# A four-layer graph network in fp32: two row broadcasts moved from TensorE to transfers, the second layer's slope and mask moved from GpSimd to VectorE

## What is computed

```python
def L0(h, adj, W, a):                      # first layer
    Wh = h @ W.T
    s1, s2 = Wh @ a[0, :128], Wh @ a[0, 128:]
    e = leaky_relu(s1[:, :, None] + s2[:, None, :], 0.2)      # a row of s2 for all nodes
    att = softmax(where(adj == 0, -inf, e))
    return att @ Wh

def L1(x, adj, W, a_1, a_2, a_12, W_1, W_2):                  # second layer
    h = x @ W
    logits = (h @ a_1).T + h @ a_2 + (h @ a_12) @ h.T
    e = leaky_relu(logits, 0.2)
    e = where(adj > 0, e, -9e15)
    return elu(x @ W_1 + (softmax(e) @ x) @ W_2)

def L2(x, adj, ...):                       # third layer: attention with 4 heads of 32
    scores = q @ k.T * scale;  attn = softmax(where(adj | eye, scores, min))
    return relu((attn @ v) @ Wo + bo)

x = layernorm(x + L0(x)); x = layernorm(x + L1(x))
x = layernorm(x + L2(x)); x = layernorm(x + L3(x))            # L3: gated relation layer
```

## Time and profile before

| | |
|---|---|
| time, median of 3 runs | 496.18 us (496.12 to 496.77) |
| the profiled execution | 496.9 us, of it the span 495.0 us |
| PE busy | 468.4 us, 95% of the span, 3872 matmuls |
| DVE busy | 410.8 us, 83% |
| ACT busy | 428.0 us, 86% |
| POOL busy | 370.6 us, 75% |
| DMA | 26.9 MB, the 16 engines 18% busy |
| granted TensorE clock | 0.988 of full speed on average |

### The profile page before, as it was taken

How to read it: one execution, slowest core, us unless ns; L and a number is a source line. 1 busy time by engine, 2 the same in 40 slices (tenths; PEclk the granted TensorE clock), 3 DMA queues, 4 the chain that set the end, 5 groups by cost and what they waited for, 6 DMA issues and landing times. The chain is left out here.

```text
span 495.0 us, 13988 instructions
## 1 busy us (share of the span) xinstructions
PE 468.4 (95%) x3872; PEld 402.3 (81%) x3872; DVE 410.8 (83%) x1605; ACT 428.0 (86%) x1261; POOL 370.6 (75%) x736
## 2 busy tenths in 40 slices
PE   6968999999999999999999999999999999999793
PEld 5756778988888888988888888888888888877572
DVE  5657898998888998898888988898898989876653
ACT  3558999999999999999999999999999999988750
POOL 1365576788888888888888888888888888986523
PEclk9989999999999999999999999999999999999997
DMA  7211111122112221222112221221123100000011
GB/s 219 74 44 44 44 54 52 40 63 66 40 48 66 66 66 54 54 66 63 36 56 66 65 60 51 66 65 43 45 66 87 34 23 13 23 24 23 22 45 44
DMA packets 40222, 26.93 MB, mean 54 GB/s; under 512 B 2641, under 2 KB 39889, under 8 KB 40146
## 3 DMA queue, kind: packets, MB, share of 16 engines
q1 hardware_dynamic: 40146, 26.03, 18.4%
HBM read 17.63 MB, written 8.39 MB: 53 GB/s over the span
## 5 line engine op out<-in xcount | busy, mean ns | idle before, releaser
L1211 POOL TENSOR_SCALAR x<-y,minus_mean,rstd 128x128 f32<-128x128 f32 x244 | 144.8, 601 | 6.8 <-issue 5.1
L788 ACT ACTIVATE p<-p,nmax 128x256 f32<-128x256 f32 x256 | 128.5, 530 | 0.4 <-DVE nmax L981 0.4
L981 DVE CUSTOM_DVE_ANT_0 p<-ps,neg 128x256 f32<-128x256 f32 x256 | 90.7, 420 | 2.3 <-PE ps L564 2.3
L1193 POOL TENSOR_TENSOR rstd<-ve,minus_half 128x2 f32<-128x2 f32 x128 | 91.1, 712 | 0.0
L575 PE MATMUL ps<-ident,p 128*128 128x128 f32 x512 | 78.0, 275 | 4.1 <-DVE nmax L981 3.4
L1186 POOL TENSOR_SCALAR ve<-stats 128x2 f32<-128x2 f32 x128 | 24.6, 192 | 72.3 <-DVE stats L896 64.9
L797 ACT COPY p2T<-ps 128x512 f32<-128x512 f32 x128 | 75.2, 590 | 1.3 <-PE ps L575 0.5
L575 PEld LDWEIGHTS ps<-ident,p 128*128 128x128 f32 x512 | 61.3, 143 | 9.3 <-DVE nmax L981 4.0
L788 ACT ACTIVATION_READ_ACCUMULATOR p<-p,nmax 128x1 f32 x256 | 56.1, 219 | 0.0
L896 DVE BATCH_NORM_STATS2 stats<-y 128x6 f32<-128x256 f32 x128 | 54.1, 423 | 1.5
L1175 POOL TENSOR_TENSOR relu<-relu,neg 128x512 f32<-128x512 f32 x32 | 37.1, 1161 | 21.1 <-ACT relu L757 21.1
(11 more groups left out here) (130 smaller groups left out, 1210.3 us busy)
## 6 DMA issues: line engine op xcount, KB each, us to landing
adj_in<-in_adj_dram SPq DMA_DIRECT2D x32, 256.0 KB, 3.0
xT<-in_xT_dram SPq DMA_DIRECT2D x32, 128.0 KB, 2.1
x_in<-in_x_dram SPq DMA_DIRECT2D x32, 128.0 KB, 2.1
x_aside<-x SPq DMA_DIRECT2D x32, 128.0 KB, 2.1
out_dram<-x SPq DMA_DIRECT2D x32, 128.0 KB, 2.9
l_w<-in_l_w_dram SPq DMA_DIRECT2D x1, 257.0 KB
l_w<-in_l_w_dram SPq DMA_DIRECT2D x1, 256.0 KB
first_w<-in_first_w_dram SPq DMA_DIRECT2D x1, 129.0 KB, 2.2
```

The source lines that it names most:

```text
L788: last = nc.scalar.activation(p2(n)[:, k, a, :], p2(n)[:, k, a, :], ACT.Exp, bias=nmax2(n)[:, k, a:a + 1], scale=-1.0, accum_out=sum2(n)[: ...
L981: last = nc.vector.tensor_tensor_reduce(p2(n)[:, k, a, :], bank("sc2", n, a)[:, k * N:(k + 1) * N], neg2(n)[:, k, :], -1.0, HIGHEST, ALU.a ...
L1193: nc.gpsimd.tensor_tensor(rstd[layer](n), ve[layer](n), minus_half[:, :], ALU.pow)\
L1211: last = nc.gpsimd.tensor_scalar(dst[:, k, 0:D], y_t[layer](n)[:, k, :], minus_mean[layer](n)[:, k:k + 1], rstd[layer](n)[:, k:k + 1], ALU ...
```

## The change

`s2_rows` and `c_s2` are left for the first three graphs only (`PE_ROWS`). From the fourth on, `proj0` gives one more column (0.2 times s2), `s2_out` writes both columns to DRAM and `s2_in` reads them back to all 128 partitions as pairs, and `e0` reads both rows from SBUF, 8 bytes apart. `rs_rep` goes: `rs_rows` is one transpose of the 8 columns of `rsum2`, `c_rs` evicts 8 partitions x 128, and `rs_in` (two DMAs from SBUF to SBUF) spreads each row over 32 partitions. In layer 2, `relu1` writes 0.2 z, the new step `lk1` on DVE forms max(z, 0.2 z) in place, `rmask1` on POOL goes, and `e1` adds the mask from SBUF. `neg1` holds the mask itself and is freed by `e1`; the logits' bank is freed by `lk1`. Two semaphores of the norms are merged into one. `xw0` gets 4 buffers (3 before) and `s2row` 3 (2 before). The numbers of `PLAN` are new for all steps, and the flag of a rare case is computed at the very end.

```diff
-    "sync": [("ld_xT", 6707), ("ld_adj", 7906), ("ld_w", 8043), ("ld_x", 8602), ("aside", 16291), ("store", 19013)],
+    "sync": [("ld_xT", 8117), ("ld_adj", 8710), ("ld_w", 8972), ("s2_out", 9299), ("s2_in", 9427), ("ld_x", 10713),
+        ("rs_in", 14787), ("aside", 17215), ("store", 19815)],
...
+PE_ROWS = 3
...
+    **{step: (0, PE_ROWS) for step in ("s2_rows", "c_s2")},
+    **{step: (PE_ROWS, 0) for step in ("s2_out", "s2_in")},
...
-    "z1": [("b", "e1_ready")],
+    "z1": [("b", "leaky_ready")],
...
-        s2row = ring("s2row", [N])
+        s2row = ring("s2row", [N, 2])
...
-        rs_rep = ring("rs_rep", [T, D], of="rs_row")
+        rs_turned = ring("rs_turned", [P], of="rs_row")
...
+            def rs_in(n):
+                sp.wait_ge(sem("rs_sb"), n + 1)
+                free(sp, "rs_row", n, "onT_sb")
+                for k in range(T):
+                    sp.dma_start(rs_row(n)[:, k * P:(k + 1) * P],
+                                 rs_turned(n)[k * HEADS:(k + 1) * HEADS].rearrange("h (a i) -> h a i", a=1)
+                                 .broadcast_to((HEADS, DK, P))).then_inc(sem(f"rs_in{n % RING['rs_row']}"), 16)
+
+            def s2_out(n):
+                sp.wait_ge(sem("wh_sb"), n + 1)
+                sp.dma_start(s2_dram[n].rearrange("(t p) c -> p t c", p=P), xw0(n)[:, :, 1:3])\
+                    .then_inc(sem(f"s2_out{n % 2}"), 16)
+
+            def s2_in(n):
+                sp.wait_ge(sem(f"s2_out{n % 2}"), 16 * ((n - PE_ROWS) // 2) + 16)
+                free(sp, "s2row", n, "e0_ready")
+                sp.dma_start(s2row(n).rearrange("p j c -> p (j c)"),
+                             s2_dram[n].rearrange("(a j) c -> a (j c)", a=1).broadcast_to((P, 2 * N)))\
+                    .then_inc(sem(f"s2_in{n % RING['s2row']}"), 16)
...
-                    last = pe.matmul(o[:, k * (D + 2):(k + 1) * (D + 2)], xT0(n)[:, k * P:(k + 1) * P], w0_w[:, :],
+                    last = pe.matmul(o[:, k * (D + 3):(k + 1) * (D + 3)], xT0(n)[:, k * P:(k + 1) * P], w0_w[:, :],
...
-                pe.wait_ge(sem("rs_rep_ready"), n + 1)
-                for k in range(T):
-                    last = pe.transpose(o[:, k * P:(k + 1) * P], rs_rep(n)[:, k, :], ident[:, :])
-                last.then_inc(sem("rs_ps"), 1)
+                pe.wait_ge(sem("rsum2_ready"), n + 1)
+                pe.transpose(o[0:T * HEADS, 0:P], rsum2(n).rearrange("p t h -> p (t h)"), ident[:, :])\
+                    .then_inc(sem("rs_ps"), 1)
...
-                nc.scalar.activation(relu(n).rearrange("p t n -> p (t n)"), bank("z1", n), ACT.Relu,
-                                     scale=(1.0 - SLOPE) / SLOPE).then_inc(sem("relu_ready"), 1)
+                nc.scalar.activation(relu(n).rearrange("p t n -> p (t n)"), bank("z1", n), ACT.Copy,
+                                     scale=SLOPE).then_inc(sem("relu_ready"), 1)
...
+            def lk1(n):
+                dve.wait_ge(sem("z_ps"), n + 1)
+                dve.wait_ge(sem("relu_ready"), n + 1)
+                o = bank("z1", n).rearrange("p (t n) -> p t n", t=T)
+                nc.vector.scalar_tensor_tensor(out=relu(n), in0=o, scalar=1.0, in1=relu(n), op0=ALU.mult, op1=ALU.max)\
+                    .then_inc(sem("leaky_ready"), 1)
+
             def e1(n):
-                dve.wait_ge(sem("rmask_ready"), n + 1)
+                dve.wait_ge(sem("leaky_ready"), n + 1)
+                dve.wait_ge(sem("neg1_ready"), n + 1)
                 free(dve, "p1", n, "pT_ps1")
-                o = bank("z1", n)
-                for k in range(T):
-                    last = nc.vector.tensor_tensor_reduce(p1(n)[:, k, :], o[:, k * N:(k + 1) * N], relu(n)[:, k, :],
-                                                          -SLOPE, HIGHEST, ALU.add, ALU.min, nmax1(n)[:, k:k + 1])
+                for k in range(T):
+                    last = nc.vector.tensor_tensor_reduce(p1(n)[:, k, :], relu(n)[:, k, :], neg1(n)[:, k, :],
+                                                          -1.0, HIGHEST, ALU.add, ALU.min, nmax1(n)[:, k:k + 1])
...
-                nc.gpsimd.tensor_tensor(relu(n), relu(n), neg1(n), ALU.add).then_inc(sem("rmask_ready"), 1)
```

More of the change, by code:

```diff
@@ L170, in build @@
         bo_row = sb("bo_row", [P, D])
-        w0_w = first_w[:, 0:D + 2]
+        w0_w = first_w[:, 0:D + 3]
         l1_part = sb("l1_part", [P, 2, P])
@@ L254, in build @@
         x3_dram = nc.dram_tensor("x3_aside", (B, P, T * D), F32, kind="Internal").ap()
+        s2_dram = nc.dram_tensor("s2_rows", (B, N, 2), F32, kind="Internal").ap()
         x_v = t["x"].rearrange("b (t p) d -> b p t d", p=P)
@@ L355, in _ @@
             sp.dma_start(first_w[:, :], t["first_w"]).then_inc(sem("w0_loaded"), 16)
-            run("sync", {"ld_adj": ld_adj, "ld_xT": ld_xT, "ld_x": ld_x, "ld_w": ld_w, "aside": aside, "store": store})
+            run("sync", {"ld_adj": ld_adj, "ld_xT": ld_xT, "ld_x": ld_x, "ld_w": ld_w, "rs_in": rs_in, "s2_out": s2_out, "s2_in": s2_in, "aside": aside, "store": store})
             for s in range(RING["x4"]):
@@ L679, in setup @@
                 nc.scalar.mul(w0_w[:, 0:1], ps[:, 0, 0:1], 1.0 - SLOPE)
-                nc.scalar.copy(w0_w[:, 1:2], ps[:, 0, 1:2]).then_inc(sem("weights_ready"), 1)
+                nc.scalar.copy(w0_w[:, 1:2], ps[:, 0, 1:2])
+                nc.scalar.mul(w0_w[:, 2:3], ps[:, 0, 2:3], SLOPE).then_inc(sem("weights_ready"), 1)
             def c_prep_a(n):
@@ L712, in c_proj0 @@
                 free(act, "xw0", n, "agg_ps0")
-                nc.scalar.copy(xw0(n)[:, :, 0:D + 2],
-                               bank("proj0", n)[:, 0:T * (D + 2)].rearrange("p (t d) -> p t d", t=T))\
+                nc.scalar.copy(xw0(n)[:, :, 0:D + 3],
+                               bank("proj0", n)[:, 0:T * (D + 3)].rearrange("p (t d) -> p t d", t=T))\
                     .then_inc(sem("wh_sb"), 1)
@@ L719, in c_s2 @@
                 free(act, "s2row", n, "e0_ready")
-                nc.scalar.mul(s2row(n), bank("s2_rows", n)[:, 0:N], SLOPE).then_inc(sem("s2_sb"), 1)
+                nc.scalar.mul(s2row(n)[:, :, 1], bank("s2_rows", n)[:, 0:N], SLOPE).then_inc(sem("s2_sb"), 1)
             def c_rs(n):
                 act.wait_ge(sem("rs_ps"), n + 1)
-                free(act, "rs_row", n, "onT_sb")
-                nc.scalar.copy(rs_row(n), bank("rs_rows", n)[:, 0:N]).then_inc(sem("rs_sb"), 1)
+                if n >= RING["rs_row"]:
+                    act.wait_ge(sem(f"rs_in{n % RING['rs_row']}"), 16 * T * (n // RING["rs_row"]))
+                rows = slice(0, T * HEADS)
+                nc.scalar.copy(rs_turned(n)[rows, :], bank("rs_rows", n)[rows, 0:P]).then_inc(sem("rs_sb"), 1)
             def exp0(n):
@@ L899, in e0 @@
             def e0(n):
-                dve.wait_ge(sem("s2_sb"), n + 1)
+                if n < PE_ROWS:
+                    dve.wait_ge(sem("s2_sb"), n + 1)
+                    row = bank("s2_rows", n)[:, 0:N]
+                else:
+                    dve.wait_ge(sem(f"s2_in{n % RING['s2row']}"), 16 * ((n - PE_ROWS) // RING["s2row"]) + 16)
+                    row = s2row(n)[:, :, 0]
                 free(dve, "p0", n, "pT_ps0")
                 for k in range(T):
-                    last = nc.vector.scalar_tensor_tensor(out=p0(n)[:, k, :], in0=bank("s2_rows", n)[:, 0:N],
-                                                              scalar=xw0(n)[:, k, 0:1], in1=s2row(n),
-                                                              op0=ALU.add, op1=ALU.max)
+                    last = nc.vector.scalar_tensor_tensor(out=p0(n)[:, k, :], in0=row, scalar=xw0(n)[:, k, 0:1],
+                                                          in1=s2row(n)[:, :, 1], op0=ALU.add, op1=ALU.max)
                 last.then_inc(sem("e0_ready"), 1)
@@ L993, in onT2 @@
                 dve.wait_ge(sem("agg_ps2"), n * HEADS + HEADS)
-                dve.wait_ge(sem("rs_sb"), n + 1)
+                dve.wait_ge(sem(f"rs_in{n % RING['rs_row']}"), 16 * T * (n // RING["rs_row"] + 1))
                 free(dve, "onT", n, "wo_ps")
@@ L1059, in _ @@
                 "masks": masks, "neg1": neg1_, "eq1": eq1_, "flag_a": flag_a, "flag_b": flag_b, "e0": e0, "m0": m0, "s0": s0, "r0": r0, "y0": y0,
-                "b0": lambda n: moments(0, n), "e1": e1, "r1": r1, "h1": h1, "y1a": y1a, "y1b": y1b,
+                "b0": lambda n: moments(0, n), "lk1": lk1, "e1": e1, "r1": r1, "h1": h1, "y1a": y1a, "y1b": y1b,
                 "b1": lambda n: moments(1, n), "e2a": lambda n: e2(0, n), "e2b": lambda n: e2(1, n), "r2": r2,
@@ L1226, in _ @@
             run("gpsimd", {
-                "neg2": neg2_, "rmask1": rmask1, "rs_rep": rs_rep_,
+                "neg2": neg2_,
                 "var0": lambda n: variance(0, n), "rsq0": lambda n: rsqrt(0, n), "norm0": lambda n: norm(0, n),
```

44 lines of the change are left out of this document (18 added, 26 removed), and 36 rows, old and new, of tables (PLAN, RING).

## The result

The changed kernel takes **527.44 us** (523.8 to 529.35) where the kernel before took 496.48 us on the same chip: ratio 1.0614, 95% interval 1.0553 to 1.0674. It is 31 us slower; 8 us faster was forecast. The profiled execution took 529.35 us, its span is 527.6.

The account below looks back on a forecast made before the run. PE's own instructions were taken as the bound in the full pipeline. Span 495.0 - 8.6 (PE) + 0.8 (DVE hold-ups) - 0.5 (start) + 0.4 (end) = 487.1 us, time 488.3 us; range 484.8 to 495.2, chance 0.80.

Parts of the forecast that it names:

- Cost: none.: POOL and SP: the new DMAs land in time, 14.6 us cover against some 5 and 9.2 against about 3; no cost.
- The rival of a gain lost whole: Period back to 14.0 us because e0 waits for s2_in or onT2 for rs_in; 495.5 to 497 us, chance 0.06.
- The range: Forecast times from 484.8 to 495.2 us, holding the forecast, DVE second bound and the narrow transpose rival; chance 0.80.
- The two ends: Start -0.5 us; at the end the last onT2 needs a landing of 2.1 us: +0.4, 0 to +2.
- What PE loses: On PE, fewer and narrower transposes less a wider proj0: -8.6 us in all, a period of 13.67 us.
- narrow transpose: rs_rows on PE taken at 0.11 us; rival: 0.27 us, giving back 4.3 us, 492.6 us, chance 0.10.
- DVE: DVE's work per graph: busy 13.20 us, some 13.4 with small gaps, under PE's 13.67; +0.8 us for occasional hold-ups.
- DVE as second bound: Rival: with the hexp wait left, DVE needs 13.96 us; periods 13.80 to 13.97 give 491 to 495 us, chance 0.15.
- Slower than PE was, by two SBUF reads: Rival: e0 and e1 read SBUF twice while POOL reads it; 497.5 to 513 us, by the rule 528; chance 0.09.
- The start, -0.5: Before PE's first exp1 wait, lk1 takes 0.66 us where rmask1 on POOL took 1.16: -0.5 us.
- The sum: Span 495.0 - 8.6 + 0.8 - 0.5 + 0.4 = 487.1 us, giving a time of 488.3 us.

Follow-up runs that it names:

- e4: The changed kernel with three places of SP's table moved: s2_out directly in front of rs_in, s2_in directly behind it; 496.59 us, ratio 0.9997.
- e5: e4 with the row of 1/sum of the last three graphs made by POOL and PE as before; 488.61 us, ratio 0.9834 to the kernel before.
- e11: The changed kernel in its own order, with the row of 1/sum of only the last three graphs repeated by PE; 520.4 us, ratio 1.0466.
- e12: The changed kernel with the two transfers of rs_in issued by GpSimd instead of SP, SP's other steps unmoved; 494.84 us, ratio 0.995.

## Why the prediction was wrong, point by point

- **The step that failed** is the one on POOL and SP that ends in "Cost: none." It costs 31 us (527.4 to 496.6 by three places of SP, e4). It had two errors. The terms: landings were taken as 2 x 2.1 us from `xT`, a transfer of another shape with little in its way; measured were some 3.6 and 4.2 for the row of s2 and, at the end, 6.46 for `rs_in`, and 2.4 us for each issue behind it, 0.4 before. The reasoning weighed more: the 14.6 us from `c_proj0` to `e0` were held against the length of two landings, as if they could start when `c_proj0` is done. They start when SP gets there, and SP stood in `rs_in` for `c_rs`. The sentence before "Cost: none" names all of that queue, what stands in `rs_in` and what behind, but follows it only to the load of `xT`, not to `s2_out`.
- **The rival of a gain lost whole** had the right place (`e0` waits for `s2_in` behind SP's waits), with 0.06, but its price was capped at a period of 14.0, as if nothing could be later than before. A loop has no such cap: 1.3 us per graph beyond 13.62 and a time of 527, not 497. The range ended at 495.2, 0.2% below the time before, and left this rival out altogether; without the cap it would have had to reach far above the time before.
- **"The two ends", +0.4, 0 to +2,** measured +8 (e5 against e4) or +7 (e11 against the change). The mechanism was named, a landing on the last chain, and mis-sized: 6.46 us instead of 2.1, on the chain of the changed kernel for two graphs instead of one, and a lower clock behind it, which no term had (4.6 of the 8 us by the traces of e4 and e5).
- **What PE loses** was right: period forecast 13.67, measured 13.62 (e4, e5, e12); narrow transpose 0.11 forecast, 0.11 measured. That rival is out.
- **DVE** was right: busy 13.20 us per graph forecast, measured 13.02 (267.59 us in 20.56 periods of 13.62 in e4). `lk1` takes 0.69 (0.66 taken), `e1` has a median of 0.418 (0.46 taken), `e0` of 0.484 in the changed kernel and 0.514 in e5 (0.55). DVE as second bound is out with e4: PE full at 13.62.
- **Slower than PE was, by two SBUF reads,** forecast 528 for a wait of a whole norm in each of four instructions, after the rule of the Trainium skill (SBUF — State Buffer, Who interferes with whom), and the result is 527. That is chance: in e4 and e12 the same four instructions stand beside the same norms and the period is 13.62. A number that fits proves no mechanism, and here it would have misled. The mutual hold-up as such is in the traces. `e0` took 0.466 to 0.484 us in all 64 executions before; in the changed kernel four of them beside `neg2` took 1.37 to 1.38, one of them in this piece of the timeline (two executions, which together take 0.88 at 228.71):

```profile
333.01 1.30 POOL L1210 TENSOR_TENSOR neg<-neg,not_eye 128x512 bf16<-128x512 bf16 x1
333.22 1.76 DVE L937 SCALAR_TENSOR_TENSOR p<-s2row,xw 128x256 f32<-128x256 f32 x2
```

Beside the norms one execution each of `e0` and `e1` took 0.59 to 0.66 us in most periods of e4, 0.1 to 0.2 longer than alone. That makes 0.3 us per graph where 1.8 had been reckoned, and DVE had room for it.
- **The start, -0.5,** can't be told apart: PE is busy for 46.3 of its first 60 us against 47.8, with some transposes less to do, and no run changes the start alone.
- **The sum.** With the two failed terms taken out by hand, e5 has a span of 485.8 and a time of 488.6 us (487.65 in the profiled execution), where the forecast said 487.1 and 488.3. The forecast describes e5, not the changed kernel; that the two agree to a microsecond is in part luck, since e5's period is 0.05 us shorter than forecast.

## What to carry to other kernels

An in-order queue ties together everything that stands in it. For a transfer that is new, don't ask only whether its landing fits between producer and consumer: write the queue down step by step, see what each step waits for, and follow the chain until it returns to itself. If it does, divide its length by the periods it spans; if that is over the period of the busiest engine, it is the new bound, and one place moved or another queue undoes it. And at the end of a pipeline a transfer costs its whole latency: keep the old way for the last graphs.
